# Decoder layer, first two blocks: the prologue of the cross attention is placed among the last row parts of the first stage, and keys are scaled on GpSimd

## What is computed

```
x = layernorm(x + self_attention(x))        # 32 heads of 16, ALiBi bias, causal, biases on both projections
x = layernorm(x + cross_attention(x, ctx))
x = layernorm(x + ffn(x))                   # 16 blocks of 32 -> 128 -> 32 with a permutation, exact GELU

def cross_attention(latents, context):
    kv = concatenate([context, latents], axis=1)               # 768 rows
    q = rms_norm(heads(latents @ Wq, 32), q_norm_w)            # 32 query heads of 128
    k = rms_norm(heads(kv @ Wk, 8), k_norm_w)                  # 8 key heads of 128
    v = heads(kv @ Wv, 8)
    probs = softmax(q @ k.T / sqrt(128))                       # four query heads share a key head
    return (probs @ v) @ Wo
```

## Time and profile before

| | us |
|---|---|
| median of 3 runs (lowest, highest) | 878.85 (878.78, 880.15) |
| the profiled execution | 879.56 |
| its span | 877.7 |
| TensorE busy in the span | 835.2 (95%) |
| VectorE busy | 567.0 (65%) |
| GpSimd busy | 509.0 (58%) |
| ScalarE busy | 466.5 (53%) |

### The profile page before, as it was taken

The page is one execution under the profiler, slowest core; times in us unless marked ns, Lnnn a source line. Parts: engine busy times, 40 slices in busy tenths (PEclk is TensorE's granted clock), DMA queues, the critical chain, the costliest instruction groups (busy, mean ns, idle before and its releaser), DMA issues. The chain is left out here.

```text
span 877.7 us, 15163 instructions
## 1 busy us (share of the span) xinstructions
PE 835.2 (95%) x4841; PEld 699.1 (80%) x4841; DVE 567.0 (65%) x1539; ACT 466.5 (53%) x988; POOL 509.0 (58%) x660
## 2 busy tenths in 40 slices
PE   7999998899898989999999999999999999999976
PEld 5777776677676878888888888888888888888763
DVE  4376675677454656676777667677667767767544
ACT  5666653555233545555556456555555545555353
POOL 2666763565212866756765775675676576445830
PEclk9999999999998989999999999999999999999989
DMA  7604232111123422121122121122121102000011
GB/s 231 180 23 133 76 101 78 55 56 49 49 85 107 175 66 66 39 65 67 37 66 66 36 66 66 36 66 66 36 66 66 36 1 77 2 0 1 0 25 49
DMA packets 48463, 56.23 MB, mean 64 GB/s; under 512 B 4622, under 2 KB 29724, under 8 KB 48412
## 3 DMA queue, kind: packets, MB, share of 16 engines
q1 hardware_dynamic: 48412, 55.59, 20.5%
HBM read 41.95 MB, written 13.63 MB: 63 GB/s over the span
## 5 line engine op out<-in xcount | busy, mean ns | idle before, releaser
L1090 POOL TENSOR_SCALAR prob<-prob,x_rinv 128x768 f32<-128x768 f32 x128 | 116.3, 909 | 173.0 <-DVE x_rinv L1272 173.0
L1214 ACT ACTIVATE pT_hi<-bank 128x512 fp32r<-128x512 f32 x192 | 114.4, 598 | 95.0 <-PE bank L1450 94.4
L1190 ACT ACTIVATE prob<-bank,x_nm,q_rms 128x768 f32<-128x768 f32 x128 | 127.1, 993 | 50.8 <-DVE x_nm L1266 50.3
L1263 DVE TENSOR_REDUCE x_mx<-bank 128x1 f32<-128x768 f32 x128 | 122.1, 954 | 24.1 <-PE bank L1399 23.9
L1330 DVE TENSOR_TENSOR pT_lo<-bank,pT_hi 128x512 fp32r<-128x512 f32 x192 | 130.3, 679 | 7.7 <-ACT pT_hi L1214 6.3
L1450 PE MATMUL bank<-ident,prob 128*128 128x128 f32 x768 | 116.4, 274 | 3.5 <-POOL prob L1090 3.4
L1450 PEld LDWEIGHTS bank<-ident,prob 128*128 128x128 f32 x768 | 95.4, 141 | 16.3 <-POOL prob L1090 4.7
L394 ACT ACTIVATE s_self<-s_self,nm_self 128x128 f32<-128x128 f32 (+1 forms) x128 | 57.0, 447 | 66.5 <-DVE nm_self L510 66.5
L48 PE MATMUL bank<-pT_hi,xv_hi 128*128 128x512 f32 x192 | 86.6, 451 | 0.9 <-DVE pT_lo L1330 0.8
L50 PE MATMUL bank<-pT_hi,xv_lo 128*128 128x512 f32 x192 | 75.8, 395 | 0.0
L49 PE MATMUL bank<-pT_lo,xv_hi 128*128 128x512 f32 x192 | 75.4, 393 | 0.0
(11 more groups left out here) (202 smaller groups left out, 2037.3 us busy)
## 6 DMA issues: line engine op xcount, KB each, us to landing
wo_raw<-in_Wo SPq DMA_DIRECT2D x8, 1024.0 KB, 5.4
wq_raw<-in_Wq SPq DMA_DIRECT2D x7, 1024.0 KB, 5.4
v_by_head<-v_st SPq DMA_DIRECT2D x12, 512.0 KB, 3.2
kT_by_head<-kT_st SPq DMA_DIRECT2D x12, 512.0 KB, 3.2
xk_raw<-kT_by_head SPq DMA_DIRECT2D x16, 384.0 KB, 3.1
xv_raw<-v_by_head SPq DMA_DIRECT2D x16, 384.0 KB, 3.1
wq_raw<-in_w_attn SPq DMA_DIRECT2D x12, 256.0 KB, 4.1
xk_raw<-in_ctx SPq DMA_DIRECT2D x8, 256.0 KB, 2.7
```

The source lines that it names most:

```text
L1090: nc.gpsimd.tensor_scalar(prob[:, s, :], prob[:, s, :], rinv[:, s:s + 1], 1.0, ALU.mult, ALU.mult)\
L1190: nc.scalar.activation(prob[:, s, :].rearrange("p (a e) -> p a e", a=2), bank[:, at:at + 2, 0:HALF], ACT.Exp, bias=nm[:, s:s + 1], scale=q ...
L1214: nc.scalar.activation(pT_hi[:, a, :], bank[:, turn.bank[s, what, a], :], ACT.Copy)\
L1263: nc.vector.reduce_max(mx[:, s:s + 1], bank[:, at:at + 2, 0:HALF], AX.XY)\
```

## The change

- **Prologue into the first stage.** The transposes of the first two query tiles (`QT`), the split of the first head's keys (`KS`), the power of the queries (`QM`), the first four score tiles (`XS`) with maximum and shift (`XM`), exponential (`XE`) and normalisation (`XI`), and the third query product (`Q` 2) become entries of `ORDER`, set among the row parts (10, 3) to (12, 4). The second block's prologue keeps one query product; its GpSimd queue starts with the values.
- **Rows spread otherwise.** `Y` is made in two halves, layer norm, `X1` and `XT` of the third and fourth row tile stand further behind each other (`XT` 3 behind row part (10, 3)), `W` 8 now stands right behind `Y` 3 and ahead of row part (10, 0), and the first two query products stand behind the parts (10, 3) and (10, 4) instead of row 11 and (12, 4). One row part goes from the twelfth unit of the self attention to the last.
- **Keys scaled on GpSimd.** The multiply of a key half by `k_inv` goes from VectorE (line 560) to GpSimd, right behind the power (24 times).
- **Values copied by two engines.** VectorE still copies the first half of a row's values; the second half is copied by ScalarE at the next row's part 0 (12 times, semaphore `vg_late`).
- SP loads the first values at row 10. The tensors that both blocks now use are placed by a new function `handed_on`, so that they lie over those of the first stage that are no longer needed; it issues nothing.

```diff
...
-        if c < NQ - 4:
+        if c < NQ - 5:
...
+    parts(1)
     order += [("PV", NQ // 2 - 1), ("A", NQ // 2 - 1)]
...
-    parts(1 + (q + 1) % 2)
-    order += [("Y", 2), ("Y", 3), ("LN", 2)]
     parts(1)
-    order += [("X1", 2), ("LN", 3)]
+    order += [("Y", (2, 0)), ("Y", (2, 1))]
     parts(1)
-    order += [("XT", 2), ("X1", 3)]
-    parts(max(0, (B * CT + 2) * PARTS - q))
-    order += [("XT", 3), ("W", 8)]
-    parts(ROWS * PARTS - q)
-    order.append(("Q", 0))
-    parts(5)
-    order.append(("Q", 1))
...
+    order += [("X1", 2), ("Y", (3, 0)), ("XT", 2), ("Y", (3, 1)), ("LN", 3), ("W", 8)]
...
+    order.append(("KS", 0))
+    for j in range(UT):
+        order.append(("XS", j))
+        parts(1)
+        order.append(("XM", j))
+        if j > 0:
+            order.append(("XI", j - 1))
+        order.append(("XE", j))
+    parts(1)
+    order.append(("XI", UT - 1))
...
     assert q == ROWS * PARTS + 5
...
+                    sp.wait_ge(v_store, 16 * n)
+                    sp.dma_start(k.v_raw[:, 0, :], k.v_dram[0, :, 0:KEYS]).then_inc(k.v_in[0], 16)
+                sp.wait_ge(vg_out, n + 1)
+                sp.wait_ge(vg_late, n + 1)
...
+                        pool.wait_ge(kinv_made, 2 * n + g + 1)
+                        nc.gpsimd.tensor_tensor(k_rows[:, w, :], k_rows[:, w, :], k_inv[:, w].rearrange("p (h a) -> p h a", a=1)
+                                                .to_broadcast([P, GH, HD]), ALU.mult).then_inc(knrm_made, 1)
...
+                elif what == "XI":
+                    pool.wait_ge(k.rinv_made, a + 1)
+                    nc.gpsimd.tensor_scalar(k.prob[:, a, :], k.prob[:, a, :], k.rinv[:, a:a + 1], 1.0, ALU.mult, ALU.mult)\
+                        .then_inc(k.prob_made, 1)
...
+                if r == 0 and n >= 1:
+                    act.wait_ge(g_ps, 4 * n)
+                    if n >= 2:
+                        act.wait_ge(v_store, 16 * (n - 1))
+                    nc.scalar.activation(v_st[:, GH:KVH, :].rearrange("p h e -> p (h e)"),
+                                         bank[:, bank_of("part", (n - 1, 6)), :], ACT.Copy).then_inc(vg_late, 1)
...
+                elif what == "KS":
+                    act.wait_ge(k.k_in[0], 16)
+                    for p in range(2):
+                        nc.scalar.activation(k.k_hi[:, 0, half_keys(p)], k.k_raw0[:, half_keys(p)], ACT.Copy)\
+                            .then_inc(k.first_hi, 1)
+                elif what == "XE":
+                    act.wait_ge(k.nm_made, a + 1)
+                    at = 2 * (a % 2)
+                    nc.scalar.activation(k.prob[:, a, :].rearrange("p (a e) -> p a e", a=2), bank[:, at:at + 2, 0:HALF],
+                                         ACT.Exp, bias=k.nm[:, a:a + 1], scale=k.q_rms[:, first_tile(a)[2]],
+                                         accum_out=k.rsum[:, a:a + 1]).then_inc(k.exp_made, 1)
...
-            def take_values(n, g):
-                dve.wait_ge(g_ps, 4 * n + g + 3)
+            def take_values(n):
+                dve.wait_ge(g_ps, 4 * n + 3)
                 if n >= 1:
                     dve.wait_ge(v_store, 16 * n)
-                nc.vector.tensor_copy(v_st[:, GH * g:GH * (g + 1), :].rearrange("p h e -> p (h e)"),
-                                      bank[:, bank_of("part", (n, 4 + 2 * g)), :]).then_inc(vg_out, 1)
+                nc.vector.tensor_copy(v_st[:, 0:GH, :].rearrange("p h e -> p (h e)"),
+                                      bank[:, bank_of("part", (n, 4)), :]).then_inc(vg_out, 1)
 
...
-                if r in (5, 7):
-                    g = r // 2 - 2
-                    w = slice(GH * g, GH * (g + 1))
-                    dve.wait_ge(kinv_made, 2 * n + g + 1)
-                    nc.vector.tensor_tensor(k_rows[:, w, :], k_rows[:, w, :], k_inv[:, w].rearrange("p (h a) -> p h a", a=1)
-                                            .to_broadcast([P, GH, HD]), ALU.mult).then_inc(knrm_made, 1)
+                    take_values(n)
...
+                elif what == "KS":
+                    for p in range(2):
+                        dve.wait_ge(k.first_hi, p + 1)
+                        nc.vector.tensor_tensor(k.k_lo[:, 0, half_keys(p)], k.k_raw0[:, half_keys(p)],
+                                                f32(k.k_hi[:, 0, half_keys(p)]), ALU.subtract).then_inc(k.k_split, 1)
...
+                    if a == 2:
+                        pe.wait_ge(k.exp_made, 3)
+                    at = a % 2
                     for i in range(KT):
...
+                elif what == "QT":
+                    pe.wait_ge(q_rows_out, a + 1)
+                    drained("QT", a)
+                    for g in range(GRP):
+                        last = nc.tensor.transpose(bank[:, bank_of("QT", a), tokens(g)], k.q[:, a, g * HD:(g + 1) * HD], ident[:])
+                    last.then_inc(k.ring_full, 1)
+                elif what == "XS":
+                    g, tt, _ = first_tile(a)
+                    if a == 0:
+                        pe.wait_ge(k.ring_out, 2)
+                        pe.wait_ge(k.k_split, 2)
+                        pe.wait_ge(ss_part, 2 * GRP)
+                    elif a >= 2:
+                        pe.wait_ge(k.exp_made, a - 1)
+                    for a_hi, k_part, start, stop in ((k.qT_hi, k.k_hi, True, False), (k.qT_hi, k.k_lo, False, False),
+                                                      (k.qT_lo, k.k_hi, False, True)):
+                        for p in range(2):
+                            last = nc.tensor.matmul(bank[:, 2 * (a % 2) + p, 0:HALF], a_hi[:, g, tokens(tt)],
+                                                    k_part[:, 0, half_keys(p)], start=start, stop=stop)
+                    last.then_inc(k.s_full, 1)
...
             sp.wait_ge(k.v_store, 16 * ROWS)
-            load_values(0, 0)
             sp.wait_ge(k.k_store, 16 * ROWS)
             load_keys(1, 0)
...
-            pool.wait_ge(first_ms, 1)
-            nc.gpsimd.tensor_tensor(q_inv[:, columns(0)], q_ms[:, columns(0)], minus_half[:, columns(0)], ALU.pow)\
-                .then_inc(first_inv, 1)
             for p in range(2):
                 values(0, p, 0, p)
-            for j in range(UT):
-                norm(j, j)
...
-            for tt in range(2):
-                split_queries(tt, tt, first_bank(tt))
-            act.wait_ge(k_in[0], 16)
-            for p in range(2):
-                w = slice(p * HALF, (p + 1) * HALF)
-                nc.scalar.activation(k_hi[:, 0, w], k_raw[0][:, w], ACT.Copy).then_inc(first_hi, 1)
-            for j in range(UT):
-                exponentials(j, 0, j, 2 * j)
...
-            for tt in range(2):
-                transposed_queries(tt, 0, tt, first_bank(tt), first=True)
-            pe.wait_ge(ring_out, Turn.BEFORE)
-            pe.wait_ge(k_split, 2)
-            for j in range(UT):
-                scores(j, 0, j, 2 * j, early=True)
-            for r in range(2):
-                pe.wait_ge(exp_made, r + 1)
-                w = slice((2 + r) * P, (3 + r) * P)
-                for m in range(KT):
-                    last = three_passes(nc, bank[:, FIRST_Q[r], :], k.x1_hi[:, m, w], k.x1_lo[:, m, w],
-                                        wq_hi[:, m, :], wq_lo[:, m, :], m == 0, m == KT - 1)
-                last.then_inc(first_q_ps, 1)
+            pe.wait_ge(exp_made, UT)
+            w = slice(3 * P, 4 * P)
+            for m in range(KT):
+                last = three_passes(nc, bank[:, FIRST_Q[1], :], k.x1_hi[:, m, w], k.x1_lo[:, m, w],
+                                    wq_hi[:, m, :], wq_lo[:, m, :], m == 0, m == KT - 1)
+            last.then_inc(first_q_ps, 1)
...
```

207 lines of the change are left out of this document (131 added, 76 removed).

## The result

The changed kernel ran at 872.49 us in the median of four runs (871.8 to 872.98), beside 879.5 for the kernel before; the ratio is 0.9916 with a 95% interval of 0.9894 to 0.9938. So the change is worth 7 us, where 4.7 had been forecast; faster it is, and inside the range.

The account below looks back on a forecast made before the run. TensorE was taken to bound the kernel, busy 835.2 of 877.7 us. Body -2.2, tail +4.9 and behind the seam -7.4 sum to -4.7 us: 874.9 us profiled, 874.2 against the median, range 868 to 881.

Parts of the forecast that it names:

- What bounds it: Whole kernel: TensorE, busy 835.2 of 877.7 us; only its idle time and its time at the lower clock can be won.
- Part 1, the body: First stage's body: VectorE's relief wins 3.2 of 7.4 us idle, GpSimd's added work costs 1.0; together -2.2 us.
- the sign that I had named for the body: Body: TensorE's idle time up to the end of the attention near 5 us.
- The copies on ScalarE: First stage: half of the value copies cost nothing while ScalarE waits for shifts, with one exception in the tail.
- the exception that I named: Tail: ScalarE's copy of row 9's values stands behind four roundings of Wq; a wait of 3.0 us.
- Part 2, the tail: Tail up to the seam: 6.2 us of waits go, work moves in, new waits arise; the seam comes 4.9 us later.
- Wait ahead of row part (10, 0): Tail: TensorE waits 3.0 us for ScalarE's copy of row 9's values, which frees the bank.
- Part 3, behind the seam, -7.4: Seam to tile waits: GpSimd's queue sets the length, 24.6 us instead of 32.0, with Wq landing at 11.3.
- What was "not touched": The rest of the kernel, from 319.62 us on, which the change was said not to touch.
- The relief is worth more: Rival, body: every VectorE wait goes (-7.4, not -2.2) and the 3.0 us wait brings no slow clock; 867.2 us, chance 0.18.
- Moved, not hidden: Rival, seam: its holes reappear at its ends, Wq lands late, the body gains nothing; 880.6 us, chance 0.17.
- GpSimd late: Rival, first stage: each multiply delays normalisations and biases behind it by up to 1.3 us; 885.2 us, chance 0.15.

Follow-up runs that it names:

- row_part_back: The kernel of `all_three` with one row part back from the last unit of the self attention to the twelfth; 861.49 us.
- queue_longer: The changed kernel with one more power, into an unread scratch tile, in GpSimd's queue behind the seam; 873.36 us.
- tiles_before_weights: The changed kernel with the next unit's four tiles set among the query weights in GpSimd's queue behind the seam, not behind them; 868.84 us.
- all_three: The changed kernel with row 9's values copied ahead of the weight roundings, first keys split one row part earlier, tiles set among query weights; 864.46 us.
- before_keys_moved: The kernel before with one edit, the multiply of the key halves on GpSimd right behind the power; 876.18 us.
- both_back: The changed kernel with the multiply of the keys and the second half of the value copies both back on VectorE; 880.48 us.

## Why the prediction was right, and where it was not

**Direction and most of the mechanism held; the sum was 2 us short, and the term of the body was near its number by luck.** Forecast -4.7, profile to profile -6.6, medians -7.0. By its own steps:

- *What bounds it.* TensorE's lost time, and nothing else: every variant's time follows TensorE's waits and its clock. The waits of the earlier trace rows went as told.
- *Part 1, the body, -2.2.* The net body came out at -2.1 in the first profile and, with the lower clock in it, at -0.6 in the second, and the first is a sum of two errors. The multiply on GpSimd was worth 3.3 to 4.4 us and not 2.2: I had taken 3.2 of the 7.4 us and charged 1.0. The multiply took 1040 ns, not the 1291 of the earlier trace rows. Against it stand the two new waits of 1.23 us, which the prediction did not have. They come from the one row part moved from the twelfth to the last unit: with it, a transpose of keys stands between the product with the values and the next transposes, and these run into the bank of that product. `row_part_back` shows it, 1.8 us in the body. I had read the order of the tail and taken that of the body for unchanged. So the sign that I had named for the body missed: TensorE's idle time from 50 us to the last transpose of probabilities was to be near 5 us and was 8.0 (8.4 before), and VectorE ended every wait above 0.3 us in it. And the wait that I had taken as the example of VectorE's load, the 1.30 us of the earlier trace rows, did not shrink at all.
- *The copies on ScalarE* at nothing: nearly right for the body, where they made the wait of the earlier trace rows 0.48 us longer. At the exception that I named they cost less than on VectorE, 2.76 against 4.92 us.
- *Part 2, the tail.* Wait ahead of row part (10, 0): 3.0 told, 2.76 measured, from the order on ScalarE. Wait ahead of the scores: 1.8 told, 1.57. Seam: 0.5 told, 0.32. Slow clock: 1.8 told, 3.1 in one profile and none in the next. The seam came 6.3 us later from the body's end on; my 4.9 counted the 1.06 us of the earlier trace rows with the tail, and with that on the other side it is 6.0.
- *Part 3, behind the seam, -7.4.* This is the term that was mis-sized: -9.5 and -10.2 in the two profiles. The structure was right, and `queue_longer` shows that the queue's length ends the hole one for one (1.64 us more in the queue, 1.67 more of wait). But I had Wq land 11.3 us behind the seam with GpSimd waiting; it did not wait. The keys came 5.4 behind the seam (5.9 told), so the queue took 23.1 and the scores went on 23.3 us behind the seam, not 24.6 (the terms named add up to 24.3; 0.3 stands in it without a source). From the last product to these scores 7.3 us passed, 5.9 of them waits, within the 7 to 9 told. And the stretch at the lower clock behind the hole was 0.8 us shorter (from scores to the unit's transpose 6.2 us, 7.0 before), where I had kept it.
- *What was "not touched"* gained 2.8 us. All profiles with the new prologue have 487.5 or 487.6 us from Wo to Wo, before had 489.4. A wait of 0.57 us at 427.76 is part of it. The rest is a drift of a tenth here and there, and its cause stays open. The last 1.0 us goes with the clock: over the first 6.9 us of the last block it was 0.57 before and 0.76 now. Of the 1.7 at the start, 1.6 are the first eight products at about half the pace (see the end); the start was anywhere from 33.6 to 36.5 us in the 14 profiles.

**The rivals.** *The relief is worth more* had the right sign, but not its ground, that every wait in the body goes. *Moved, not hidden* is what the prologue without the engine moves is: with both taken back, nothing is left of the gain, and its late Wq was in that profile (1.35 us). *GpSimd late* did not happen, but it was nearer than its 0.15 said. I had computed a threshold of 0.2 us for each of the 24; a second added microsecond costs 0.26 each. The rule of the Trainium skill's GPSIMD Engine Reference, section 4.1, to give elementwise work on a tile to VectorE, speaks of the operation's own length. The trace agrees with the direction but shows a factor of 1.5 (1040 against 695 ns) where the page has about 2; the 1040 ns are near the estimate of 1.1 us by the 2.6 cycles per element of its section 3. The kernel's time went the other way: VectorE released TensorE's waits, and GpSimd had room for one such operation.

**Where the headline's gain went.** Four score tiles, eight transposes and one query product left the stretch behind the seam, and the seam to Wo stretch is 9.5 us shorter; but 7.7 us of that is TensorE's own work, which moved ahead. What could be won was the holes, and of the 10.6 us (6.2 and 4.4) that went in tail and seam, the change put 4.7 back as three new waits, up to 3.1 of slow clock, and a longer hole behind the first unit. The two engine moves are not additions to the prologue but its condition here: with them undone the times are those of before.

## What to carry to other kernels

When a prologue is moved under other work, price the operations that stand ahead of each moved piece in its own engine's list: both new waits in the tail were a copy or a rounding queued behind work that was less urgent, and setting it one place earlier gave back about 4 and 1 us. In a program whose order is one shared list, moving one filler shifts the phase of all that follow; look for new neighbours that share a buffer. And before an engine is given more work, add a piece of that length twice, the second into a scratch tile: it tells the slack that the busy share (61% here) does not.

## What the runs showed of the hardware

The same wait of 2.76 us, at the same place, stands in seven profiles. In one (the changed kernel's first) it was followed by 7.3 us at a granted clock of 0.58, in the other six, one of them of the same kernel, by 1.00. These six had a stretch at 0.66 to 0.71 over 5 us some 80 us earlier instead, behind the 1.78 us wait in the body, where the first had 1.00. The three profiles that have the 1.78 us wait and not the 2.76 had 1.00 behind the first and up to the first scores. So what a wait costs by the clock, 0, 1.5 or 3 us here, could not be read from its length, and what decides between the two places stays open. Behind the 4.92 us wait the clock was 0.72 over the next 7.3 us in both profiles that have it.

What the lower clock costs depends on what comes behind it: ahead of a wait that something else ends it cost nothing, behind one 1.6 us (`tiles_before_weights` and `all_three`).

The kernel's first products show such a difference too: they started 0.43 us apart in the changed kernel and 0.23 in the kernel before, and this made the start 1.6 us later, though the granted clock over these few microseconds reads 1.00 in both. Changed:

```profile
9.70 0.76 PE L48 MATMUL bank<-x_hi,w_hi 128*128 128x512 f32 x1 [2.10 <-DVE w_lo L560]
10.26 0.63 PE L49 MATMUL bank<-x_lo,w_hi 128*128 128x512 f32 x1
10.69 0.63 PE L50 MATMUL bank<-x_hi,w_lo 128*128 128x512 f32 x1
```

Before:

```profile
9.66 0.47 PE L48 MATMUL bank<-x_hi,w_hi 128*128 128x512 f32 x1 [2.10 <-DVE w_lo L499]
9.97 0.39 PE L49 MATMUL bank<-x_lo,w_hi 128*128 128x512 f32 x1
10.20 0.40 PE L50 MATMUL bank<-x_hi,w_lo 128*128 128x512 f32 x1
```

The transfer of 1 MB of Wq behind the seam took 6.0 to 7.2 us in eleven profiles and 8.1 in three (`before`, `before_keys_moved`, `both_back`). Only in `both_back` did it hold GpSimd up, for 1.35 us: in the other two GpSimd came to the weights over 18 us behind the seam.
